# The first two of a step's four low weight halves on GpSimd instead of VectorE, and the row scatters one round later

## The reference, cut to what matters

```python
x = x + xattn(layernorm(x), ctx, ctx, igate_w, igate_b, fgate_w, fgate_b, out_w)   # 32 sequences x 128 tokens x 256
x = x + ffn(layernorm(x), gate_w, w1, b1, w2, b2)

# ffn: 8 experts, two of them for each token
gate_scores = softmax(xf @ gate_w); topk_scores, topk_idx = top_k(gate_scores, 2); topk_scores /= sum(topk_scores)
h = gelu(einsum('td,edf->etf', xf, w1) + b1[:, None, :])      # w1: 8 x 256 x 1024
y = einsum('etf,efd->etd', h, w2) + b2[:, None, :]            # w2: 8 x 1024 x 256
out = einsum('kt,ktd->td', topk_scores.T, y[topk_idx.T, tok])
```

## Time and profile before

| | |
|---|---|
| time, median of 3 runs | 666.69 us |
| the three runs | 665.88, 666.69, 667.96 us |
| span of the profiled execution | 672.2 us (no other time of it is given) |
| instructions in it | 20373 |
| attention stage in it | to about 255 us |
| mean granted TensorE clock | 0.981 of full speed |
| low halves on VectorE | 32 instructions |

### The profile page before, as it was taken

How to read it: one execution, slowest core, us unless ns; L and a number is a source line. 1 busy time by engine, 2 the same in 40 slices (tenths; PEclk the granted TensorE clock), 3 DMA queues, 4 the chain that set the end, 5 groups by cost and what they waited for, 6 DMA issues and landing times. The chain is left out here.

```text
span 672.2 us, 20373 instructions
## 1 busy us (share of the span) xinstructions
PE 626.9 (93%) x6736; PEld 533.2 (79%) x6737; DVE 489.8 (73%) x1330; ACT 323.3 (48%) x767; POOL 187.1 (28%) x185
## 2 busy tenths in 40 slices
PE   1799998999889899999999999999999999999985
PEld 1567876778677668988989898988889898988774
DVE  2457988979889898985889866757675757666562
ACT  2668888777878746543332232323232323232321
POOL 3000003231323315135345332313141323233112
PEclk9899999969999999999999999999999999999998
DMA  4534537654644636333374423233232323133100
GB/s 139 156 106 148 160 94 231 188 189 144 207 152 137 199 103 208 77 70 78 66 221 93 68 40 61 43 56 46 46 52 44 57 39 64 35 65 53 21 4 1
DMA packets 55036, 66.55 MB, mean 99 GB/s; under 512 B 5472, under 2 KB 50720, under 8 KB 54832
## 3 DMA queue, kind: packets, MB, share of 16 engines
q1 hardware_dynamic: 41552, 48.13, 24.1%
q0 software_dynamic: 13296, 17.32, 14.1%
q10 hardware_dynamic: 112, 0.08, 0.1%
HBM read 41.50 MB, written 24.92 MB: 99 GB/s over the span
## 5 line engine op out<-in xcount | busy, mean ns | idle before, releaser
L1038 ACT ACTIVATE decay_slots<-scores,b_turned 128x256 f32<-128x256 f32 (+1 forms) x312 | 124.4, 451 | 257.4 <-PE scores L1519 244.9
L1519 PE MATMUL scores<-x_slots,w_halves 128*128 128x256 f16 (+1 forms) x1872 | 203.3, 264 | 0.8 <-issue 0.8
L1519 PEld LDWEIGHTS scores<-x_slots,w_halves 128*128 x1872 | 173.4, 98 | 23.3 <-issue 1.4
L641 POOL DMA_INDIRECT expert_rows<-xf_rows,slot_i x64 | 66.7, 1042 | 224.1 <-issue 114.8
L1533 PE MATMUL pv<-w_halves,decay_slots 128*128 x864 | 97.7, 273 | 0.0
L663 POOL DMA_INDIRECT out_rows<-v_centred_and_one,row_ids x36 | 57.8, 1605 | 138.8 <-DVE v_centred_and_one L2111 96.1
L1533 PE MATMUL gate_bank<-w_halves,q_and_k_halves 128*128 x840 | 95.0, 273 | 0.0
L1533 PEld LDWEIGHTS pv<-w_halves,decay_slots 128*128 128x128 f16 x864 | 84.1, 98 | 10.5 <-issue 0.3
L1533 PEld LDWEIGHTS gate_bank<-w_halves,q_and_k_halves 128*128 128x128 f16 x840 | 81.8, 98 | 10.1
L663 POOL DMA_INDIRECT out_rows<-work,row_ids x35 | 55.3, 1580 | 112.1 <-DVE work L2111 84.7
L1257 PEld LDWEIGHTS pv<-v_centred_and_one,decay_slots 128*128 128x128 f32 x512 | 64.5, 197 | 1.6
(11 more groups left out here) (257 smaller groups left out, 845.5 us busy)
## 6 DMA issues: line engine op xcount, KB each, us to landing
weight_stage<-in_L_ffn_w SPq DMA_DIRECT2D x32, 512.0 KB
x_slots<-in_x SPq DMA_DIRECT2D x16, 512.0 KB
weight_stage<-expert_rows SPq DMA_DIRECT2D x30, 272.0 KB
ctx_slots<-in_ctx SPq DMA_DIRECT2D x8, 512.0 KB
out_rows<-x_slots SPq DMA_DIRECT2D x8, 512.0 KB
v_centred_and_one<-expert_rows SPq DMA_DIRECT2D x9, 272.0 KB
expert_rows<-v_centred_and_one SPq DMA_DIRECT2D x9, 272.0 KB
expert_rows<-xf_rows,slot_i POOLq DMA_INDIRECT x64
```

The costliest lines, as they stand in the source:

```text
L641: pool.indirect_dma_start(table, bass.IndirectOffsetOnAxis(ap=sloti[:, step[1], j, k:k + 1], axis=0), xfn[:, step[1], j, :], None, bounds_ ...
L1038: ins = act.activation(hf[:, f * R:f * R + tr.rows(0)], ps_s[:, q, n * R:n * R + tr.rows(0)], ACT.Gelu, bias=b1T[:, bass.ds(expert, 1), f] ...
L1519: ins = pe.matmul(o, w, xh[:, tr.slot(0) % 2, b, k, 0:tr.rows(0)], start=(n == 0), stop=(n == 3 * KC - 1))
```

## The change

Low halves 0 and 1 of every step leave VectorE. GpSimd makes them, each with two instructions: the staged piece is multiplied by 64 in place, and the high half is subtracted from it. Halves 2 and 3 stay on VectorE. The semaphore `s_lo` becomes two, one for each staging slot. GpSimd's `body` scatters the rows of the step before `last`, in the order: low half 0 of `nxt`, row 0 of the scatter, low half 1, rows 1 to 3. GpSimd's `first_steps` makes the first two low halves of S0, S1 and S2 and scatters nothing; after the rounds the scatter of S5 follows.

```diff
                     if n >= 2 or some(step, 1):
-                        sp.wait_ge(s_lo, g * 4 + (n - 1))
+                        sp.wait_ge(s_lo[half], g * 2 + q)
                         sp.sem_inc(s_held, 1)
...
+                def weights_low(step, n):
+
+                    g, half, q = number(step), n % 2, n // 2
+                    pool.wait_ge(s_hi, g * 4 + n + 1)
+                    e, k = g, q
+                    if half == 0:
+                        hi, lo = (w1s[:, bass.ds(e, 1), a, k, :].rearrange("p a f -> p (a f)") for a in range(2))
...
+                    src = stage[:, half, :]
+                    pool.tensor_scalar(src, src, W_SCALE, None, ALU.mult).then_inc(s_w64, 1)
+                    pool.wait_ge(s_w64, g * 2 + (n + 1))
+                    pool.tensor_tensor(lo, src, hi, ALU.subtract).then_inc(s_lo[half], 1)
...
                 def body(last, step, nxt, after):
-                    if last is not None:
-                        scatter(last)
+                    older = divmod(number(last) - 1, 2)
+                    weights_low(nxt, 0)
+                    scatter_ready(older)
+                    scatter_row(older, 0)
+                    weights_low(nxt, 1)
+                    scatter_row(older, 1)
+                    scatter_row(older, 2)
+                    scatter_row(older, 3)
 
                 def first_steps():
-                    scatter(S0)
+                    for step in (S0, S1, S2):
+                        for n in range(2):
+                            weights_low(step, n)
 
                 first_steps()
                 run_steps(body, pool)
+                scatter(divmod(NSTEP - 3, 2))
...
                     if after is not None:
                         next_stats(after)
-                    if nxt is not None:
-                        weights_low(nxt, 0)
                     if after is not None:
                         next_norm(after)
...
                         next_a(nxt)
-                        weights_low(nxt, 1)
                         running_max(nxt)
```

More of the change, by code:

```diff
@@ L265, in build @@
         s_hi = sem("weights_high")
-        s_lo = sem("weights_low")
+        s_w64 = sem("weights_scaled")
+        s_lo = [sem(f"weights_low{p}") for p in range(2)]
         c_dn = Chain(sem("dve_next"), DVE_NEXT)
@@ L542, in _ @@
                         sp.wait_ge(done, SLOTS_FULL[p] * SCATTERED)
-                sp.wait_ge(s_lo, 4 * NSTEP)
+                for done in s_lo:
+                    sp.wait_ge(done, 2 * NSTEP)
                 for k in range(3):
@@ L621, in _, with scatter_row, scatter_ready @@
                     pool.memset(xfn[:, p, :, D:ROW], 0.0).then_inc(s_cp, 1)
-                def scatter(step):
+                def weights_low(step, n):
[4 more added lines that the diff above has]
+                        hi, lo = (w1s[:, bass.ds(e, 1), a, k, :].rearrange("p a f -> p (a f)") for a in range(2))
+                    else:
+                        hi, lo = (w2s[:, bass.ds(e, 1), a, k * (FC // 2):(k + 1) * (FC // 2), :].rearrange("p a c d -> p (a c d)")
+                                  for a in range(2))
+                    src = stage[:, half, :]
+                    pool.tensor_scalar(src, src, W_SCALE, None, ALU.mult).then_inc(s_w64, 1)
+                    pool.wait_ge(s_w64, g * 2 + (n + 1))
+                    pool.tensor_tensor(lo, src, hi, ALU.subtract).then_inc(s_lo[half], 1)
+                def scatter_row(step, j):
+                    for k in range(2):
+                        if j:
+                            pool.wait_ge(s_sc[step[1]][k], step[0] * SCATTERED + j * 16)
+                            pool.sem_inc(s_held, 1)
+                        pool.indirect_dma_start(
+                            table, bass.IndirectOffsetOnAxis(ap=sloti[:, step[1], j, k:k + 1], axis=0),
+                            xfn[:, step[1], j, :], None, bounds_check=TABLE - 1,
+                            oob_is_err=False).then_inc(s_sc[step[1]][k], 16)
+                def scatter_ready(step):
                     g = number(step)
@@ L635, in scatter @@
                     pool.sem_inc(s_held, 1)
+                def scatter(step):
+                    scatter_ready(step)
                     for j in range(SB):
[L637 to L644, removed]
-                def body(last, step, nxt, after):
-                    if last is not None:
-                        scatter(last)
+                        scatter_row(step, j)
+                def body(last, step, nxt, after):
+                    older = divmod(number(last) - 1, 2)
[6 more added lines that the diff above has]
+                    scatter_row(older, 3)
                 def first_steps():
-                    scatter(S0)
+                    for step in (S0, S1, S2):
+                        for n in range(2):
+                            weights_low(step, n)
                 first_steps()
                 run_steps(body, pool)
+                scatter(divmod(NSTEP - 3, 2))
                 def add_rows(tr):
@@ L1705, in weights_low @@
                     dve.scalar_tensor_tensor(out=lo, in0=stage[:, half, :], scalar=W_SCALE, in1=hi, op0=ALU.mult,
-                                             op1=ALU.subtract).then_inc(s_lo, 1)
+                                             op1=ALU.subtract).then_inc(s_lo[half], 1)
                 def c_of(step, j):
@@ L1931, in first_steps @@
                     next_norm(S0)
-                    weights_low(S0, 0)
                     constants()
-                    weights_low(S0, 1)
                     gate_bias(S0)
@@ L1948, in first_steps @@
                     gate_bias(S1)
-                    weights_low(S1, 0)
                     next_norm(S2)
@@ L1954, in first_steps @@
                     c_of(S0, 3)
-                    weights_low(S1, 1)
                     running_max(S1)
@@ L1969, in first_steps @@
                     x1_norm(S0)
-                    weights_low(S2, 0)
                     log_f(S2)
@@ L1978, in first_steps @@
                     split(S2)
-                    weights_low(S2, 1)
                     weights_low(S2, 2)
```

## The result

The changed kernel took 682.65 us (median of four runs, 681.64 to 688.27) where the kernel before, run beside it, took 666.72 (median of four too): a ratio of 1.0258, 95% interval 1.0207 to 1.031, so slower by 16 us. The forecast was 680. In the file after, lines behind the new GpSimd code stand 32 further down: L1679 is now L1711, L1714 is L1746, L1820 is L1852.

The account below looks back on a forecast made before the run. PE is full from 75 to 102 us; in the rounds PE and VectorE are both close to full. Terms 0 + 11.0 + 1.0 + 1.5 = 13.5 us, added to the 666.7 median, gave 680 us, range 662 to 694.

Parts of the forecast that it names:

- the waits ahead of `next_norm` and of the running maximum: VectorE's waits in a round, expected to grow to 1.5 and 1.0 us as it comes early to both.
- TensorE's wait for `c_of`: At a round's start, expected to grow from 0.4 to some 2.6 us.
- Taken from VectorE: Sixteen instructions, 18.1 us in all, thought covered by waits: 0 taken, 4.5 us gain at the other end.
- at 197.82 in any case: When ScalarE's first guess, which VectorE awaits after low half 0, was said to come; so half 0 gains nothing.
- Added on GpSimd: Time of one half there: 1.04 + 0.2 + 1.9 = 3.1 us, against 1.13 on VectorE.
- Half 0 at `records`: GpSimd's two instructions hold VectorE's two-operand instructions at `records`, delaying `c_of`: 2.2 us a round, 11.0 us in five.
- Half 1: Runs on GpSimd from 198.8 to 202.0, holding the split's start 0.2 us, covered at 203.81: no cost.
- The 0.2 us of cover at `h_norm`: VectorE's 0.21 us wait for ScalarE before `h_norm` at 203.81, said to cover half 1's hold.
- The prologue: Six halves of the first steps; a subtraction may hold VectorE's gate instruction at 23.27: 1.0 us, between 0 and 1.8.
- The scatter: Rows 1 to 3 go out later behind half 1, but are covered by 2 to 2.5 us: no cost.
- The rival of a GpSimd too slow for its scatter: With halves of 6 us, late rows delay `x1_normed` and the expert stage's loads: 6.6 us, 673, chance 0.08.
- The clock: PE's 2.2 us wait for `c_of` lowers the granted clock: half a fall, 1.5 us, between 0 and 6.2.

Follow-up runs that it names:

- order_only: The kernel before with all halves still on VectorE, only the scatter beginning one round later: 0.9987, 667.0 us.
- subtract_only: The changed kernel without GpSimd's multiplication, the high half subtracted from the unscaled piece: 1.0235 to the kernel before, 682.3 us.
- one_operand: The changed kernel with GpSimd's subtraction replaced by a one-operand pass copying the scaled piece to the low half: 1.0261 to the kernel before, 683.1 us.
- multiply_only: The changed kernel without GpSimd's subtraction, 64 times the piece written to the low half: 1.0046 to the kernel before, 668.4 us.

## Why the prediction was right, and where not

The direction, the size (16 us for 13.5) and the kind of cause, GpSimd's passes holding VectorE up, were right. The sum was right by terms that were wrong one by one, so that it came so near is luck. Its signs are as mixed: rounds of 30 us came (29.73), and the waits ahead of `next_norm` and of the running maximum came near (1.30 and 0.66 us for 1.5 and 1.0), but TensorE's wait for `c_of` is 0.76 us in four rounds for the forecast's 2.6, and `records` takes 0.4 us more, not 2.2.

- *Taken from VectorE*, 0 with 4.5 at the other end: without the two halves of the rounds, and with the later scatter, the kernel is 2.5 us faster, so 0 was too low for the two together, the range right. The guess does not come "at 197.82 in any case": VectorE goes on with it 4.78 us after the start of the round of before (197.86 less 193.08), 4.31 with the scatter alone moved, 3.78 with the halves left out as well. Which half the gain comes from was not tried by leaving one out.
- *Added on GpSimd*, 3.1 us a half: 5.0. The step that failed is pricing one operand by the select's 0.84 ns a column; the multiplication took 2.80 us for 1024 columns, 2.7 ns a column. The subtraction was near: 1.9 forecast, 2.18 measured. The Trainium skill's figure for an add (GPSIMD Engine Reference, section "Performance versus the Vector engine"), halved to an estimate of 2.25 us, was nearer still. The Trainium skill also says there, in the section "Engine selection", that one operand goes roughly at line rate; here the pass with one operand is slower than the one with two, and the measurement decides. Where the forecast leans on "select and copies", the trace of before has selects alone; it holds no copy on GpSimd.
- *Half 0 at `records`*, 11.0 us: putting it back gives 0.5%, some 3 us, not resolved from zero. Because the multiplication is 1.8 us longer, the subtraction starts when `records` is over, but for the one ahead of the first round. The length of a hold was right: with the multiplication left out, so that the subtraction starts at the entry to `records`, it held VectorE for 1.5 to 1.9 us in four rounds. How much of that kernel's 682 us is the hold and how much the clock is not separated.
- *Half 1*, 0 us: this is the term that carried the largest part of the loss, 1.4%, some 9 us. The forecast had it done at 202.0, beside the start of the split; it starts behind row 0 and takes 5 us, so its end (210.30) lies 2.0 us after the start of the split's subtraction. The 0.2 us of cover at `h_norm` were no match for holds of 2.3 to 3.7 us on the split in four of the five rounds (2.5 in the one shown).
- *The prologue*, 1.0 us: 0.9%, some 6 us. It was priced by one gate instruction of the first step; what came was 2.10 us at the second step's log-sigmoid, 2.7 at its split, SP's load of x 1.1 us late, and the fall of the clock after TensorE's wait at 62.01. No kernel made these six halves alone on GpSimd.
- *The scatter*, 0: confirmed alone (0.9987), by the time; its rounds are 0.5 us shorter. The rival of a GpSimd too slow for its scatter did not decide here, though with halves of 5 us the cover was thin: SP's first loads of the expert stage came at 258.37 after waiting 4.0 us for the last rows, and TensorE's first turn of them came with the last `c_of` (262.2 and 261.99), as before (251.1 and 251.14).
- *The clock*, 1.5: not separated, but probably too small. The mean granted clock of the profiled attention stage is 0.95 after and 0.96 before, and 0.97 with the halves left out of the rounds, but order_only too shows 0.95 at the time of before. Single runs say more: 0.968 to 0.983 in the four of the changed kernel (mean 0.977), 0.979 to 0.991 in thirteen of the kernel before (mean 0.985). Over 682 us the difference is some 5 us, an estimate of the most that it cost, and the parts above contain it. In the same way it comes to 9 us in subtract_only (0.974 for 0.987), 12 in one_operand (0.971 for 0.988) and none in multiply_only (0.987 for 0.987).

What is shown: which parts cost, and that GpSimd's passes cost 0.4 to 5% by where they fall and what is queued behind them. What stays open is how much of each loss comes by way of the clock, and how GpSimd's multiplication lets VectorE through: see the last section.

## What to carry to other kernels

Before giving GpSimd elementwise work beside a busy VectorE, lay both timelines side by side with GpSimd's true durations, and look at what VectorE runs in each of those microseconds: in these runs a pass did not lengthen instructions that read PSUM, reductions or statistics, and held up, for as much as its whole length, casts, scalar operations and two-operand arithmetic. Ask also what is queued behind the slower engine: here SP's loads (x in the first step, the context in another version) stood in order behind the slot that GpSimd freed late. And find what the spared time is worth by leaving the work out first, with everything else as in the change; 0.4%, the later scatter's share included, was all there was to win in the rounds.

## What the runs showed of the hardware

- GpSimd's subtraction held VectorE until it ended, whatever the offset: L1711 and L1675 beside the full 2.1 us took 2.31 and 2.10 us, and a one-operand scalar operation of four columns in the subtract-only kernel up to 2.02. Never longer were the 32 `c_of` (1.22 us, one operand in PSUM), the reduction at the head of `h_norm` and the statistics. The Trainium skill, SBUF — State Buffer, section "Who interferes with whom", says that casts and scalar operations can contend with GpSimd, that instructions with two operands in SBUF contend with its reads, and that reductions never do; the forecast had used only its two-operand part. These rows agree with it.
- The multiplication did not hold everything for its whole length, as that section of the Trainium skill has it. VectorE's casts, scalar operations and two-operand instructions that came 0.05 to 0.8 us after the start of a multiplying pass went on 0.9 us after that start: L1640 ended 1.06 us after it at 138.53 and at 198.01 alike, though it had come 0.11 and 0.46 us after it. Of what came later, the small two-operand instructions from 198.12 to 198.85 passed at full speed; the cast at 199.15 waited until the end at 199.72, as did every cast and scalar operation that came between 1.7 and 2.5 us after a start. Between 1.2 and 1.7 us some casts waited (200.43 of the kernel with one operand, 1.19 us after the start) and some did not (203.50 in the same round, 1.34 us after the start of the next pass, 0.28 us). So it is not the kind of the instruction alone; what else decides is not settled.
- The hold goes the other way too: GpSimd's subtraction at 88.70, which came 0.2 us after VectorE's low half 2 (88.51, 1.23 us, both operands in SBUF), took 3.03 us where it takes 2.13.
